# A sixth slot for x, and w2 read in full rows, in a fused attention and FFN layer on eight cores

## The chip, the cores and the metric

The kernel runs on one Trainium2 chip, on its 8 cores at once. Each core works on one of the eight batch elements (4096 tokens of width 1024) with all weights, and the cores exchange nothing. The metric is device microseconds of the slowest core.

## The reference

One layer: linear attention with a norm on its output, then a quantized feed-forward net with a norm on its output, each added to its input.

```python
x = x + _layernorm(_L0_attn_ref(_layernorm(x), W_qkv, W_o))
x = x + _layernorm(_L0_ffn_ref(_layernorm(x), w1, b1, w2, b2, gamma, beta))
# attention, chunk by chunk, 16 heads of 64; k is normalized per head
qkv = x @ W_qkv
inter = einsum('bhde,bthe->bthd', S, q_c)
scores = where(causal, einsum('bthd,bshd->bhts', q_c, k_c), 0)
intra = einsum('bhts,bshd->bthd', scores, v_c)
S = S + einsum('bthd,bthe->bhde', v_c, k_c)
y = (inter + intra) @ W_o
# ffn: h = layernorm(x)*gamma+beta; out = qlinear(gelu(qlinear(h, w1, b1)), w2, b2)
def qlinear(x, w, b):
    xq, sx = act_quant(x)          # 127/max|x| of a row, rounded
    scale = 1 / mean(abs(w)); wq = clip(round(w * scale), -1, 1)
    return (xq @ wq.T) / (sx * scale) + b
```

The sizes are x 8 x 4096 x 1024, w1 4096 x 1024 and w2 1024 x 4096, all in float32. A weight can be turned into its three values only when the mean over all of it is known, so w1 and w2 are each read twice: once to be summed, once to be quantized.

## The kernel before

A core's tokens are T = 32 tiles of 128. The kernel has two phases. In the **attention phase** a loop over i = -1..31 works on three tiles at once: iteration t finishes tile t (scores, masks, `attend`, `out_proj`), projects k, q and v of tile t+1, and begins tile t+3 (`ln1`, the activation `h1`, and its transposition by DMA, `h1_tp`). The residual add `x1(t-1)` and the statistics `ln3(t-1)` of the tile before also fall in iteration t. The result of the attention half is stored to a scratch tensor in HBM (`x1s`). In the **FFN phase** a loop over the 32 tiles does ffn1 and ffn2, reads x1 back from the scratch tensor, and stores the output.

Beside the attention phase the weights w1 and w2 are prepared. Each is cut into 32 pieces of 128 x 1024 floats (512 KB). The list `plan` gives each iteration its pieces: iterations 1 to 8 only sum (five or six pieces each), 9 to 17 mix sums with the quantization of w1, 18 to 31 only quantize (three or four each, two in the last three). POOL issues the loads (`load`) and computes the lower comparison of a piece (`below`). ACT sums pieces (`piece_sum`), DVE sums some of them (`piece_vsum`) and completes each quantization (`quant_piece`), and SP issues the transposition of the quantized piece (`piece_tp`).

A piece is loaded into one of 18 buffers: two of their own (`pc`), eight that lie where w1 will stand once quantized (`pc1`), and eight where w2 will stand (`pc2`). A table that is computed when the program is built chooses the buffer that was held least recently (`held`, `where`, `prior`), and from it `load` takes the work that it must wait for. At most four loads are in flight.

The tiles of x lie in five slots, `xs[:, k % 5]`. Numbers k of 32 and more are the tiles of x1 that the FFN phase reads back. SP serves them: in iteration t it issues the store of x1 of tile t-1 (L1062), then the transposition of h1 of tile t+3 (L1021), then it waits for the landing of that store and for `ln3(t-1)` and issues the load of tile t+4 into the slot set free (L1071), and then it issues the transpositions of the iteration's quantized pieces (L1034). DVE needs tile t+4 at the start of iteration t+1, in `ln1` (L531). Before the loop SP issues the loads of tiles 0 and 1, the eight parts of wk, the rows of b1, and the loads of tiles 2 and 3 (L1050). Meanwhile POOL issues wq, wv (L1127), the eight parts of w_o (L1129), and the first pieces.

All engines run their instructions in the order in which they are written, and wait for each other through semaphores.

Of the kernel before, what the change touches and what calls it, by code (L numbers as in the profile page):

```python
# [21 lines left out]
def build(NT=4096):  # L22
# [176 lines left out]
    def before(n, h=1):  # L199
        return 2 * (n // 3) - 1 + h  # L200

    s_xld = [sem(f"x_loaded{i}") for i in range(5)]
    s_xst = [sem(f"x1_stored{i}") for i in range(5)]
# [29 lines left out]
                                            sem("ln5_r"), sem("zn"), sem("out_ready"))  # L233

# [52 lines left out]
    held = [-1] * 10 + [8] * 8  # L287
    count = [0] * 18
# [27 lines left out]

    def slot(k):
        return xs[:, k % 5]

    def loaded(k):  # L320
        return 16 * (k // 5 + 1)

    def piece_src(p):
        j = p[2]
        if p[1] == 0:
            return w1_h[j * 128:(j + 1) * 128, :]
        return (w2_h[(j // 4) * 128:(j // 4 + 1) * 128, :]
                .rearrange("p (e b n) -> p e b n", e=2, b=4)[:, :, j % 4, :])
# [4 lines left out]
    def pe_program(PE):  # L333
# [193 lines left out]
    def dve_program(V):  # L527
        def ln1(t):
            xb = slot(t)
            V.wait_ge(s_xld[t % 5], loaded(t))  # L530
# [103 lines left out]
        def front_a(t):  # L634
            V.wait_ge(s_xld[(T + t) % 5], loaded(T + t))
# [377 lines left out]
    def sp_program(SP):  # L1013
        def rows(ap, t):
            return ap[t * 128:(t + 1) * 128, :]

        def h1_tp(t):
# [19 lines left out]
        for t in range(2):  # L1037
            SP.dma_start(out=xs[:, t], in_=rows(x_h, t)).then_inc(s_xld[t], 16)
# [10 lines left out]
        for t in range(2, 4):  # L1049
            SP.dma_start(out=xs[:, t], in_=rows(x_h, t)).then_inc(s_xld[t], 16)  # L1050
# [6 lines left out]
        for i in range(-1, T):  # L1057
            t, u, f = i, i + 1, i + 3
            if t >= 1:
                n = nWO(t - 1)  # L1060
                SP.wait_ge(s_fr[n % 3], emptied(n))
                SP.dma_start(out=rows(x1_h, t - 1), in_=slot(t - 1)  # L1062
                             ).then_inc(s_xst[(t - 1) % 5], 16)
# [12 lines left out]
            for p in now[1:]:  # L1076
                piece_tp(p)
# [6 lines left out]
        SP.dma_start(out=rows(x1_h, T - 1), in_=slot(T - 1)).then_inc(s_xst[(T - 1) % 5], 16)  # L1084
        SP.wait_ge(s_xst[(T - 1) % 5], loaded(T - 1))
        SP.wait_ge(s_bn3, T)
        SP.dma_start(out=slot(T + 4), in_=rows(x1_h, 4)).then_inc(s_xld[(T + 4) % 5], 16)
# [5 lines left out]
        for t in range(T + 1):  # L1093
# [6 lines left out]
            if t >= 1:  # L1100
                SP.wait_ge(s_out, t)
                SP.dma_start(out=rows(out_h, t - 1), in_=slot(T + t - 1)
                             ).then_inc(s_ost[(t - 1) % 5], 16)
                if t + 4 < T:
                    SP.wait_ge(s_ost[(t - 1) % 5], loaded(t - 1))
                    SP.dma_start(out=slot(T + t + 4), in_=rows(x1_h, t + 4)
                                 ).then_inc(s_xld[(T + t + 4) % 5], 16)
# [8 lines left out]
        for t in range(T - 5, T):  # L1116
            SP.wait_ge(s_ost[t % 5], loaded(t))
            SP.wait_ge(s_xst[t % 5], loaded(t))


    def pool_program(GP):
# [20 lines left out]
        def load(n):  # L1142
# [13 lines left out]
            if p[1] == 1:  # L1156
                buf = buf.rearrange("p (e n) -> p e n", e=2)
# [42 lines left out]
```

## Time and profile before

| | us |
|---|---|
| median of 3 runs | 1593.38 |
| lowest, highest | 1586.81, 1600.95 |
| the profiled execution, its time | 1589.63 |
| span of its slowest core (core 4) | 1588.1 |
| span of its fastest core (core 3) | 1571.1 |
| start of the FFN loop on core 4, about | 676 |

The span is the time from a core's first instruction to its last, and 1.5 us of the profiled time lie outside it. The profile names engines PE (TensorE matmul), PEld (its weight load), DVE (VectorE), ACT (ScalarE), POOL (GpSimd) and SP (SyncE). Iteration t of the attention loop can be found in the trace by the two DVE instructions L551, the residual add of tile t-1. The attention phase takes some 43% of the time, and the FFN phase, with PE busy nearly throughout, the rest. "DMA share" in a row is the mean busy share of the core's 16 DMA engines.

### The profile page before, as it was taken

The numbers are of one execution on the slowest core, as the hardware profiler recorded it, in microseconds if no ns is written. First come the engines' busy times: TensorE is split into PE (matmuls) and PEld (weight loads), VectorE is DVE, ScalarE is ACT, GpSimd is POOL, SyncE is SP. The second block draws the span as 40 slices with busy tenths as digits, with TensorE's granted clock in tenths as the row PEclk, the third lists the DMA queues.
The fourth block names the chain that finished last, engine by engine and source line by source line (L and its number), as shares of the span: only waits on it lengthen the run. The fifth ranks groups of instructions, "written<-read, shape, count | busy, mean of one in ns | idle before, by whom it ended". The sixth has DMA issues, their size and how long they took to land.

```text
span 1588.1 us, 26545 instructions; the slowest of 8 cores (1571.1 to 1588.1 us)
## 1 busy us (share of the span) xinstructions
PE 1461.6 (92%) x8884; PEld 726.6 (46%) x8948; DVE 1148.5 (72%) x1884; ACT 634.0 (40%) x1011; POOL 267.6 (17%) x196
## 2 busy tenths in 40 slices
PE   1589797999899999699999999999999999999997
PEld 0355454555555555334444444444444444444443
DVE  7386575777788887587767777677776777767764
ACT  1268475666465555423232232332323323233231
POOL 2002113454566775200000000000000000000000
PEclk9899898999999999899999999999999999999999
DMA  9979876768686787342433523334343342343422
GB/s 226 268 183 256 204 181 177 192 172 208 165 190 156 189 179 188 96 94 61 109 74 81 101 61 98 84 80 102 62 98 84 70 112 62 96 86 64 104 49 67
DMA packets 282277, 203.65 MB, mean 128 GB/s; under 512 B 246424, under 2 KB 246424, under 8 KB 282144
## 3 DMA queue, kind: packets, MB, share of 16 engines
q1 hardware_dynamic: 261776, 131.16, 36.2%
q0 software_dynamic: 20080, 69.74, 16.8%
q8 instruction: 74, 1.21, 0.3%
q10 hardware_dynamic: 288, 1.05, 0.3%
q14 instruction: 59, 0.48, 0.1%
HBM read 112.74 MB, written 33.55 MB: 92 GB/s over the span
## 4 chain that ended last, share of the span: by engine, by line
PE 75%; DMA 7%; DVE 4%; issue 4%; DVEq 3%; ACT 3%; POOL 1%; ACTq 1%; SPq 0%; POOLq 0%
PE pz L464 28%; PE pp L452 28%; PE pp L342 8%; PE pp L360 4%; PE pp L428 4%; DMA xs<-x 2%; DMA wv<-w_qkv 2%; DMA x1s<-xs 2%; PE pp L443 1%; POOL lt L1139 1%; DVEq L533 1%; PE pp L404 1%; DVEq L737 1%; DMA kst<-w_qkv 1%; PE pp L396 1%
## 5 line engine op out<-in xcount | busy, mean ns | idle before, releaser
L452 PE MATMUL pp<-w1p,xq1f 128*128 128x512 fp8e4 x2048 | 457.2, 382 | 0.0
L464 PE MATMUL pz<-w2p,xq2f 128*128 128x512 fp8e4 x2048 | 447.1, 379 | 0.0
L464 PEld LDWEIGHTS pz<-w2p,xq2f 128*128 128x128 bf16 x2048 | 200.4, 98 | 241.6
L452 PEld LDWEIGHTS pp<-w1p,xq1f 128*128 128x128 bf16 x2048 | 195.9, 98 | 244.1 <-issue 20.1
L678 DVE TENSOR_REDUCE st<-gsb 128x1 f32<-128x1024 f32 x128 | 152.6, 1213 | 130.3 <-ACT gsb L936 130.1
L942 ACT ACT_TABLE_LOAD x31 | 39.8, 1283 | 469.8 <-DVE st L717 469.8
L1139 POOL TENSOR_SCALAR lt<-pc,st 128x1024 bf16<-128x1024 f32 x64 | 186.1, 2910 | 31.2 <-DVE wqtp L602 15.2
L936 ACT ACTIVATE gsb<-pp,st 128x1024 f32<-128x1024 f32 x128 | 142.2, 1111 | 104.8 <-PE pp L452 99.0
L342 PE MATMUL pp<-wk,h1f 128*128 128x512 bf16 x496 | 116.4, 387 | 33.0 <-DMA h1f<-h1t 22.2
L342 PE MATMUL pp<-wv,h1f 128*128 128x512 bf16 x465 | 120.7, 404 | 20.0 <-ACT qfa L893 9.6
L1158 POOL DMA_DIRECT2D pc<-w x116 | 75.0, 647 | 333.7 <-ACT pc L928 109.3
L360 PE MATMUL pp<-h1f,wq 128*128 128x256 bf16 x1024 | 119.5, 276 | 2.7 <-DMA wq<-w_qkv 2.5
L428 PE MATMUL pp<-wo,yf 128*128 128x512 bf16 x511 | 115.8, 379 | 4.9 <-DVE wo L740 3.5
L360 PEld LDWEIGHTS pp<-h1f,wq 128*128 128x128 bf16 x1024 | 101.2, 99 | 23.1 <-issue 4.1
L700 DVE TENSOR_SCALAR xq2t<-gsb 128x1024 bf16<-128x1024 f32 x128 | 88.8, 694 | 19.0 <-issue 1.0
L602 DVE SCALAR_TENSOR_TENSOR wqtp<-pc,st,lt 128x1024 fp8e4<-128x1024 f32 x64 | 89.8, 1403 | 16.0 <-POOL lt L1139 15.7
L695 DVE TENSOR_SCALAR gsb<-gsb,st 128x1024 f32<-128x1024 f32 x128 | 95.8, 748 | 2.5
L342 PEld LDWEIGHTS pp<-wk,h1f 128*128 128x128 bf16 x512 | 50.4, 99 | 92.4 <-issue 37.5
L569 DVE TENSOR_TENSOR scT<-pp,mask 128x1024 bf16<-128x1024 f32 x64 | 75.2, 1217 | 16.7 <-PE pp L371 16.6
L342 PEld LDWEIGHTS pp<-wv,h1f 128*128 128x128 bf16 x512 | 48.5, 102 | 70.7 <-issue 28.3
L710 DVE SCALAR_TENSOR_TENSOR zb<-pz,st,b2b 128x512 f32<-128x512 f32 x64 | 47.9, 748 | 40.0 <-PE pz L464 40.0
L428 PEld LDWEIGHTS pp<-wo,yf 128*128 128x128 bf16 x512 | 48.6, 98 | 58.1 <-issue 5.5
(110 smaller groups left out, 1390.3 us busy)
## 6 DMA issues: line engine op xcount, KB each, us to landing
pc<-w POOLq DMA_DIRECT2D x116, 512.0 KB, 6.7
xs<-x SPq DMA_DIRECT2D x32, 512.0 KB, 5.0
x1s<-xs SPq DMA_DIRECT2D x32, 512.0 KB, 3.6
xs<-x1s SPq DMA_DIRECT2D x32, 512.0 KB, 3.8
out<-xs SPq DMA_DIRECT2D x32, 512.0 KB, 3.0
kst<-w_qkv SPq DMA_DIRECT2D x8, 512.0 KB, 11.5
wost<-w_o POOLq DMA_DIRECT2D x8, 512.0 KB, 39.8
wq<-w_qkv POOLq DMA_DIRECT2D x1, 2048.0 KB, 22.0
```

What stands on the lines that cost most here:

```text
L342: mi = PE.matmul(half(n, h), lhsT=hf[:, kk, :], rhs=wt[:, kk, h * 512:(h + 1) * 512], start=(kk == 0), stop=(kk == 7))
L360: mi = PE.matmul(pair(n)[:, m * 256:(m + 1) * 256], lhsT=wq[:, kk, (m0 + m) * 128:(m0 + m + 1) * 128], rhs=hf[:, kk, :], start=(kk == 0), ...
L428: mi = PE.matmul(half(n, h), lhsT=yf[:, kk, :], rhs=wo[:, kk, h * 512:(h + 1) * 512], start=(kk == 0), stop=(kk == 7))
L452: mi = PE.matmul(half(n, h), lhsT=xf[:, kk, :], rhs=w1q[:, c0 // 128:c0 // 128 + 4, kk % 4, :, kk // 4], start=False, stop=(kk == 7), skip ...
L464: mi = PE.matmul(PZ[:, h * 512:(h + 1) * 512], lhsT=xq2f[:, t % 2, kk, :], rhs=w2q[:, 4 * h:4 * h + 4, kk % 16, :, kk // 16], start=(kk == ...
L569: V.tensor_tensor(out=scT[:, :, 4 * g:4 * g + 4, :], in0=pair(n).rearrange("p (a j n) -> p a j n", a=2, j=4), in1=mask[:].unsqueeze(1).uns ...
L602: V.scalar_tensor_tensor(out=wqt[:, j % 4].rearrange("p n e -> p e n"), in0=piece_buf(p)[0].rearrange("p (e n) -> p e n", e=2), scalar=c1( ...
L678: V.tensor_reduce(out=c1(amq, s), in_=gsb[:, s * 1024:(s + 1) * 1024], axis=AX.X, op=ALU.max, apply_absolute_value=True)
L695: V.tensor_scalar(out=g, in0=g, scalar1=s2, scalar2=M32, op0=ALU.mult, op1=ALU.add)
L700: V.tensor_scalar(out=xq2t[:, s * 1024:(s + 1) * 1024], in0=g, scalar1=M32, scalar2=None, op0=ALU.subtract).then_inc(s_xq2, 1)
L936: A.activation(out=gsb[:, s * 1024:(s + 1) * 1024], in_=pair(n)[:], func=AF.Gelu, scale=c1(dq1, t % 2)).then_inc(s_fr[n % 3], 2)
L1139: GP.tensor_scalar(out=lt[:, j % 2], in0=buf, scalar1=c1(nth, p[1]), scalar2=None, op0=ALU.is_lt).then_inc(s_lt, 1)
```

## The change

There are six slots for x until tile 23 is done. The sixth is the second of the two `pc` buffers, which is no buffer for pieces until then. The table `slot_no` gives each tile its slot, and `taken_from` the tile whose place it takes. Before the loop SP issues the loads of tiles 2 to 5. In the loop a tile's load is issued when the tile six before it has been stored, one iteration sooner than before, up to tile 28; from tile 29 on it is again the tile five before. Within an iteration this load now stands behind the first two transpositions of pieces. A piece of w2 is a stretch of 1024 columns, 4 KB of a row, where it was two stretches of 512 columns that lie 2048 columns apart, and ffn2 picks its chunks accordingly.

```diff
+    LEFT = 23
+    slots = [xs[:, k] for k in range(5)] + [pc[:, 1]]
+    slot_no, load_of, taken_from = list(range(6)), [0] * 6, [-1] * 6
+    oldest = 0
+    while len(slot_no) < 2 * T:
+        if oldest == LEFT:
+            assert slot_no[LEFT] == 5
+            oldest += 1
+        slot_no.append(slot_no[oldest])
+        load_of.append(0)
+        taken_from.append(oldest)
+        oldest += 1
...
     held = [-1] * 10 + [8] * 8
+    held[1] = place[plan[LEFT + 1][0]]
...
-        return (w2_h[(j // 4) * 128:(j // 4 + 1) * 128, :]
-                .rearrange("p (e b n) -> p e b n", e=2, b=4)[:, :, j % 4, :])
+        return w2_h[(j // 4) * 128:(j // 4 + 1) * 128, (j % 4) * 1024:(j % 4 + 1) * 1024]
...
-                                   rhs=w2q[:, 4 * h:4 * h + 4, kk % 16, :, kk // 16],
+                                   rhs=w2q[:, 4 * h:4 * h + 4, 4 * (kk // 8) + kk % 4, :, kk // 4 % 2],
...
+        def x_load(t):
+            SP.wait_ge(*x1_stored(t))
+            SP.wait_ge(s_bn3, t + 1)
+            for k in range(2 * T):
+                if taken_from[k] == t:
+                    SP.dma_start(out=slot(k), in_=rows(x_h, k) if k < T else rows(x1_h, k - T)
+                                 ).then_inc(loaded(k)[0], 16)
...
-        for t in range(2, 4):
-            SP.dma_start(out=xs[:, t], in_=rows(x_h, t)).then_inc(s_xld[t], 16)
+        for t in range(2, 6):
+            SP.dma_start(out=slot(t), in_=rows(x_h, t)).then_inc(s_xld[t], 16)
...
             if f < T:
                 h1_tp(f)
-            if t >= 0:
-                k = t + 4
-                if t >= 1:
-                    SP.wait_ge(s_xst[(t - 1) % 5], loaded(t - 1))
-                    SP.wait_ge(s_bn3, t)
-                SP.dma_start(out=slot(k), in_=rows(x_h, k) if k < T else rows(x1_h, k - T)
-                             ).then_inc(s_xld[k % 5], 16)
             now = [p for p in plan[t] if p[0] == "quant"] if t >= 0 else []
             for p in now[:1]:
                 piece_tp(p)
-            for p in now[1:]:
+            for p in now[1:2]:
+                piece_tp(p)
+            if t >= 1:
+                x_load(t - 1)
+            for p in now[2:]:
                 piece_tp(p)
...
+            if not used and where[p][0] == 1:
+                GP.wait_ge(*x1_stored(LEFT))
+                GP.wait_ge(s_bn3, LEFT + 1)
```

The SP queue ahead of the loop, from the rows of b1 on (`b1w`, `b1r`: b1 and its split rows), before:

```order
5 L1046 DMA b1w<-b 1x2x512 [waits constants]
6 L1046 DMA b1w<-b 1x2x512 x3
7 L1050 DMA xs<-x 128x1024 x2
8 L1054 DMA b1r<-b1hi 1x16x64 [waits b1_split]
...
18 L1021 DMA_TRANSPOSE h1f<-h1t_53 128x8x128 [waits h1]
19 L1071 DMA xs<-x 128x1024
20 L1062 DMA x1s<-xs 128x1024 [waits pair_emptied0]
```

and with the change:

```order
5 L1076 DMA b1w<-b 1x2x512 [waits constants]
6 L1076 DMA b1w<-b 1x2x512 x3
7 L1080 DMA xs<-x 128x1024 x3
8 L1080 DMA pc<-x 128x1024
9 L1084 DMA b1r<-b1hi 1x16x64 [waits b1_split]
...
19 L1051 DMA_TRANSPOSE h1f<-h1t_53 128x8x128 [waits h1]
20 L1092 DMA x1s<-xs 128x1024 [waits pair_emptied0]
```

Tiles 4 and 5 are now asked for here, the second of them into `pc`, and the load of tile 4 that stood ahead of the first store of x1 is gone.

The SP queue in iteration 26, late in the attention phase, where the tiles have five slots again, before:

```order
125 L1062 DMA x1s<-xs 128x1024 [waits pair_emptied1]
126 L1021 DMA_TRANSPOSE h1f<-h1t_53 128x8x128 [waits h1,pe_v]
127 L1071 DMA xs<-x 128x1024 [waits x1_stored0,ln3_stats]
128 L1034 DMA_TRANSPOSE w2p<-wqtp 128x4x128 [waits piece_quantized,piece_summed]
129 L1034 DMA_TRANSPOSE w2p<-wqtp 128x4x128 [waits piece_quantized] x2
```

and with the change:

```order
131 L1092 DMA x1s<-xs 128x1024 [waits pair_emptied1]
132 L1051 DMA_TRANSPOSE h1f<-h1t_53 128x8x128 [waits h1,pe_v]
133 L1064 DMA_TRANSPOSE w2p<-wqtp 128x4x128 [waits piece_quantized,piece_summed]
134 L1064 DMA_TRANSPOSE w2p<-wqtp 128x4x128 [waits piece_quantized]
135 L1044 DMA xs<-x 128x1024 [waits x1_stored1,ln3_stats]
136 L1064 DMA_TRANSPOSE w2p<-wqtp 128x4x128 [waits piece_quantized]
```

The load of tile 30, which `ln1` needs at the start of iteration 27, has moved behind two transpositions, and the second of them waits for the iteration's second quantization on DVE. In iterations 1 to 8 no piece is quantized, so there the load stands directly behind the transposition of h1, as before, and is a load for a tile one further on.

The first loads of pieces on POOL (`pc_65` are the two buffers of their own, `pc1_66` those under w1), before:

```order
7 L1129 DMA wost_50<-w_o 128x1024 x8
8 L1158 DMA pc_65<-w1 128x1024 x2
9 L1158 DMA pc1_66<-w1 128x1024 x8
10 L1158 DMA pc_65<-w1 128x1024 x2
11 L1158 DMA pc1_66<-w1 128x1024 x7
```

and with the change:

```order
7 L1155 DMA wost_50<-w_o 128x1024 x8
8 L1185 DMA pc_65<-w1 128x1024
9 L1185 DMA pc1_66<-w1 128x1024 x8
10 L1185 DMA pc_65<-w1 128x1024
11 L1185 DMA pc1_66<-w1 128x1024 x9
```

Nine loads instead of ten find a buffer that was never used, and from the tenth on each waits for a sum.

## Rows read from the trace of the kernel before

**Rows 1.** The page: span, and busy time of each engine.

```profile
span 1588.1 us, 26545 instructions; the slowest of 8 cores (1571.1 to 1588.1 us)
PE 1461.6 (92%) x8884; PEld 726.6 (46%) x8948; DVE 1148.5 (72%) x1884; ACT 634.0 (40%) x1011; POOL 267.6 (17%) x196
```

**Rows 2.** Stretches of core 4 (columns in the first row; xN are instructions).

```profile
core 4: us, PE busy (x) PEld busy (x) DVE busy (x) ACT busy (x) POOL busy (x), PEclk, DMA share, GB/s
20.00:55.00 35.00, 13.93 (x48) 6.20 (x49) 18.80 (x25) 4.72 (x7) 7.28 (x14) 0.93 1.09 182
122.00:173.00 51.00, 42.47 (x345) 25.53 (x347) 29.20 (x48) 31.75 (x69) 11.92 (x21) 1.00 0.96 253
122.00:256.00 134.00, 111.59 (x915) 66.49 (x925) 79.43 (x130) 84.55 (x179) 26.91 (x39) 0.96 0.84 213
676.00:1588.00 912.00, 899.45 (x4280) 396.20 (x4278) 669.91 (x1165) 264.94 (x252) 0.00 (x0) 1.00 0.37 82
```

**Rows 3.** The chain that ended last, around iterations 8 and 9 (start, us, what).

```profile
231.51 8.68 DMA x1s<-xs
...
240.31 11.01 DMA xs<-x
...
251.41 0.69 DVE st L531
```

**Rows 4.** L531's waits for x on cores 3, 1, 4 (us, times); span of core 1.

```profile
  DMA xs<-x: 18.7, 8
...
  DMA xs<-x: 24.2, 7
...
  DMA xs<-x: 32.0, 8
...
core 1: 1583.3 us, clock 0.981
```

**Rows 5.** Core 4's waits from 122 to 256 us (total, times, longest), and its first one.

```profile
DVE st L531 <- DMA xs<-x: 27.9, 6, 10.8
...
6.77 0.69 DVE L531 BATCH_NORM_STATS2 st<-xs 128x6 f32<-128x512 f32 x1 [3.76 <-DMA xs<-x]
```

**Rows 6.** L551 in iterations 3 to 10 (two a tile), on cores 3, 1 and 4.

```profile
L551 DVE SCALAR_TENSOR_TENSOR xs<-pp,st,xs x16: 740/746/751, 128.6 to 260.4; 128x512 f32<-128x512 f32 x16
L551 DVE SCALAR_TENSOR_TENSOR xs<-pp,st,xs x16: 741/746/752, 129.5 to 267.8; 128x512 f32<-128x512 f32 x16
L551 DVE SCALAR_TENSOR_TENSOR xs<-pp,st,xs x16: 740/746/752, 128.6 to 273.5; 128x512 f32<-128x512 f32 x16
```

**Rows 7.** DMA issues from 122 to 256 us, KB each, median us to landing.

```profile
pc<-w POOLq DMA_DIRECT2D x38, 512.0 KB, 9.0
```

**Rows 8.** PE's start on the v projection of tile 0 (start, us, instruction, idle before).

```profile
55.03 0.58 PE L342 MATMUL pp<-wv,h1f 128*128 128x512 bf16 x1 [7.54 <-DMA wv<-w_qkv]
```

**Rows 9.** Iteration 26 in order of time.

```profile
567.52 0.33 SPq L1071 DMA_DIRECT2D xs<-x  x1
568.01 6.76 SPq L1034 DMA_TRANSPOSE w2p<-wqtp  x3
568.65 1.27 DVE L602 SCALAR_TENSOR_TENSOR wqtp<-pc,st,lt 128x1024 fp8e4<-128x1024 f32 x1
...
573.42 0.68 DVE L531 BATCH_NORM_STATS2 st<-xs 128x6 f32<-128x512 f32 x1
```

**Rows 10.** Landing of x in iterations 25 to 27; pieces of w1 (374-453 us); of w2 (459-590).

```profile
DMA to landing us min/median/max: 3.8/3.9/3.9
...
DMA to landing us min/median/max: 3.6/4.6/5.2
...
DMA to landing us min/median/max: 4.2/5.2/8.1
```

**Rows 11.** The last pieces: POOL's `below` behind its load, near the end of the phase.

```profile
638.57 3.90 POOL L1139 TENSOR_SCALAR lt<-pc,st 128x1024 bf16<-128x1024 f32 x1 [6.88 <-DMA pc<-w]
647.60 2.83 POOL L1139 TENSOR_SCALAR lt<-pc,st 128x1024 bf16<-128x1024 f32 x1 [4.42 <-DMA pc<-w]
```

More of the change, by code:

```diff
@@ L200, in before @@
         return 2 * (n // 3) - 1 + h
-    s_xld = [sem(f"x_loaded{i}") for i in range(5)]
-    s_xst = [sem(f"x1_stored{i}") for i in range(5)]
+    s_xld = [sem(f"x_loaded{i}") for i in range(6)]
+    s_xst = [sem(f"x1_stored{i}") for i in range(6)]
     s_ost = [sem(f"out_stored{i}") for i in range(5)]
@@ L233, in build, with slot, loaded, x1_stored @@
                                             sem("ln5_r"), sem("zn"), sem("out_ready"))
+    LEFT = 23
[11 more added lines that the diff above has]
+    for k in range(2 * T):
+        load_of[k] = sum(1 for j in range(k + 1) if slot_no[j] == slot_no[k])
+    def slot(k):
+        return slots[slot_no[k]]
+    def loaded(k):
+        return s_xld[slot_no[k]], 16 * load_of[k]
+    def x1_stored(t):
+        return s_xst[slot_no[t]], 16 * load_of[t]
+    def out_stored(t):
+        return s_ost[t % 5], 16 * (t // 5 + 1)
     gap, hold = 12, (7, 5)
@@ L314, in q_of @@
         return qfa[:, (t // 2) % 2, j, t % 2, :] if j < 4 else qfb[:, j - 4, t % 2, :]
[L317 to L321, printed above, removed]
     def piece_src(p):
@@ L529, in ln1 @@
             xb = slot(t)
-            V.wait_ge(s_xld[t % 5], loaded(t))
+            V.wait_ge(*loaded(t))
             V.bn_stats(out=bn1[:, 0:6], in_=xb[:, 0:512])
@@ L634, in front_a @@
         def front_a(t):
-            V.wait_ge(s_xld[(T + t) % 5], loaded(T + t))
+            V.wait_ge(*loaded(T + t))
             if t == 0:
@@ L1015, in rows @@
             return ap[t * 128:(t + 1) * 128, :]
+        def x_load(t):
+            SP.wait_ge(*x1_stored(t))
+            SP.wait_ge(s_bn3, t + 1)
+            for k in range(2 * T):
+                if taken_from[k] == t:
+                    SP.dma_start(out=slot(k), in_=rows(x_h, k) if k < T else rows(x1_h, k - T)
+                                 ).then_inc(loaded(k)[0], 16)
         def h1_tp(t):
@@ L1048, in sp_program @@
                          ).then_inc(s_b1, 16)
-        for t in range(2, 4):
-            SP.dma_start(out=xs[:, t], in_=rows(x_h, t)).then_inc(s_xld[t], 16)
+        for t in range(2, 6):
+            SP.dma_start(out=slot(t), in_=rows(x_h, t)).then_inc(s_xld[t], 16)
         SP.wait_ge(s_b1s, 1)
@@ L1062, in sp_program @@
                 SP.dma_start(out=rows(x1_h, t - 1), in_=slot(t - 1)
-                             ).then_inc(s_xst[(t - 1) % 5], 16)
+                             ).then_inc(x1_stored(t - 1)[0], 16)
             if f < T:
                 h1_tp(f)
-            if t >= 0:
-                k = t + 4
-                if t >= 1:
-                    SP.wait_ge(s_xst[(t - 1) % 5], loaded(t - 1))
-                    SP.wait_ge(s_bn3, t)
-                SP.dma_start(out=slot(k), in_=rows(x_h, k) if k < T else rows(x1_h, k - T)
-                             ).then_inc(s_xld[k % 5], 16)
             now = [p for p in plan[t] if p[0] == "quant"] if t >= 0 else []
@@ L1083, in sp_program @@
         SP.wait_ge(s_fr[n % 3], emptied(n))
[L1084 to L1087, printed above, removed]
+        SP.dma_start(out=rows(x1_h, T - 1), in_=slot(T - 1)).then_inc(x1_stored(T - 1)[0], 16)
+        x_load(T - 1)
         for s in range(4):
@@ L1102, in sp_program @@
                 SP.dma_start(out=rows(out_h, t - 1), in_=slot(T + t - 1)
-                             ).then_inc(s_ost[(t - 1) % 5], 16)
+                             ).then_inc(out_stored(t - 1)[0], 16)
                 if t + 4 < T:
-                    SP.wait_ge(s_ost[(t - 1) % 5], loaded(t - 1))
+                    assert taken_from[T + t + 4] == T + t - 1
+                    SP.wait_ge(*out_stored(t - 1))
                     SP.dma_start(out=slot(T + t + 4), in_=rows(x1_h, t + 4)
-                                 ).then_inc(s_xld[(T + t + 4) % 5], 16)
+                                 ).then_inc(loaded(T + t + 4)[0], 16)
             if v < T:
@@ L1116, in sp_program @@
         for t in range(T - 5, T):
-            SP.wait_ge(s_ost[t % 5], loaded(t))
-            SP.wait_ge(s_xst[t % 5], loaded(t))
+            SP.wait_ge(*out_stored(t))
+            SP.wait_ge(*x1_stored(t))
     def pool_program(GP):
@@ L1155, in load @@
                 GP.wait_ge(s_abs, nsum[o] + 1)
-            if p[1] == 1:
-                buf = buf.rearrange("p (e n) -> p e n", e=2)
             GP.dma_start(out=buf, in_=piece_src(p)).then_inc(s_ld, 16)
```

## The prediction

> **What bounds the kernel now.** I read the page first, then the stretches, the chain, and the waits of the one instruction that the change is about. The page says that PE is busy 92% of the span on core 4, and that the cores differ by 17 us [rows 1]. The stretches say where the rest lies. In the FFN phase PE is busy 899 of 912 us at a granted clock of 1.00, so nothing is to be had there, and nothing there changes. From 122 to 256 us PE is busy 111.6 of 134 us [rows 2]. That is the early attention phase, in which weights are summed beside it. The chain shows what the stretch waits for: the store of x1 of a tile, then the load of a new tile of x into the same slot, 8.7 and 11.0 us one after the other, then `ln1` on it, then the residual add that lets PE go on [rows 3]. The store and the load together are longer than the iteration leaves them.
>
> The size of it is read from the DVE instruction that waits, L531. Core 4 waits 32.0 us in 8 times, core 1 24.2, core 3 18.7 [rows 4]. Of core 4's, 27.9 us fall in six waits between 122 and 256 us, the longest 10.8; 3.8 are the very first load of the program, which the change leaves; the rest is 0.3 [rows 5]. So 28.2 us can go on core 4, and, taking off the same 3.8, 20.4 on core 1 and 14.9 on core 3.
>
> Is such a wait paid for one to one? The cores answer this, since they run the same program and differ in these waits. From the first residual add of iteration 3 to the last of iteration 10 core 3 takes 131.8 us, core 1 138.3 and core 4 144.9 [rows 6]. Less their waits that makes 116.9, 117.9 and 116.7 us. All three come to the same figure, so each microsecond of waiting there costs about one.
>
> **The change, part by part.**
>
> *The load an iteration sooner: -28.2 on core 4, -20.4 on core 1.* The load of a tile follows the store of the tile six before. The store is issued right behind the residual add, and lands after up to 8.7 us. From there `ln1` of the new tile is now due in the second iteration after, not the next. An iteration without waits is about 117 / 7 = 16.6 us (the 0.7 us of the second half of an add aside), and that is added to the time for the load. The load that came latest was 10.8 us late [rows 5] and would now come 5.8 us before it is needed, so all six waits of core 4 go. What is then late next is PE itself, at the 117 us above. The slowest core afterwards is not core 4 (1588.1 - 28.2 = 1559.9) but core 1 (1583.3 - 20.4 = 1562.9). I take core 1.
>
> *Two loads more ahead of the loop: +5.8.* Tiles 4 and 5 are asked for together with tiles 2 and 3, while the weights land, instead of in iterations 0 and 1. The DMA engines are full there: a share of 1.09 at 182 GB/s from 20 to 55 us [rows 2]. PE idles 7.5 us for wv, which lands at 55 us, and the chain goes through it [rows 8]. Two loads are 1.05 MB, and at 182 GB/s they take 5.8 us from the queue's other work. The wait for wv is the last to end, so it is paid in full. The bounds are 0, if wv's packets are served first, and 6.6 us or so, by a rate a tenth lower. I take 5.8, since x stood in this stretch beside wv before, and both were slow. On this the Trainium skill, in DMA: Bandwidth & Descriptors, section "Rules for kernel authors", says that DMAs issued from different engines all run on the same 16 DMA engines and interleave, so that spreading them adds no bandwidth. The row with the share of 1.09 agrees. A reader who thought that x on SP's queue could not hold up wv on POOL's would put 0 here, and reach a sum 5.8 lower.
>
> *The load behind two transpositions: +2.* Up to tile 28 the extra iteration covers it. Tiles 29 to 31 have five slots again and are loaded in iterations 25 to 27. In iteration 26 the second quantization ends at 569.9 us, and SP needs its transposition first, of three that took 6.8 us with their waits; I put one at 1.5 us. So the load is issued at 571.4 instead of 567.5, lands after 3.9 us [rows 10] at 575.3, and `ln1` at 573.4 waits 1.9 us [rows 9]. Three such waits would be 6. PE is close to being the bound there, and part of each is slack of the residual add, so I take 2 of 0 to 6. The transpositions themselves are issued a little sooner; nobody waits for that.
>
> *A piece buffer less until tile 23: +2.* The sums of iterations 1 to 8 have 7 pieces of lead where they had 8, and with five or six pieces in 16.6 us a piece is some 3 us. A load takes 9.0 us there [rows 7], so 7 pieces are enough. In iterations 17 to 20 the table of buffers gives leads of 2 to 4 pieces where it gave 4 to 7. Three or four pieces in an iteration make 4 us or more for each, and the loads take 3.6 to 5.2 us [rows 10]. Two pieces are 8 us, which still covers a load. POOL is stopped sooner by a full table, and takes DVE with it now and then: bounds 0 and 5, and I take 2.
>
> *w2 in rows of 4 KB: 0.* Pieces of w2 land after 5.2 us, of w1 after 4.6 [rows 10]. If all of the difference is due to the two half rows, each load is 0.6 us shorter. Loads are waited for only at the very end, where POOL waits 6.9 and 4.4 us for the last two [rows 11], and there DVE and PE have w1's results and the last attention tile to do. At most two times 0.6 comes out. The matmuls of ffn2 have the same shapes, so no change there.
>
> The sum on core 1: 1583.3 - 20.4 + 5.8 + 2 + 2 = 1572.7 us. With 1.5 us outside the span that is 1574.2, against 1589.6 of the same execution. The median of the runs before, 1593.4, stands 3.8 above that execution, as such waits vary from run to run. Fewer waits should leave less of that, so I add 1: **1575 us**.
>
> **The rivals.**
>
> *The DMA engines give part of it back: 1582.* The engines have a share of 0.96 at 253 GB/s from 122 to 173 us, and 0.84 over all of 122 to 256 us, where 213 GB/s x 134 us = 28.6 MB pass [rows 2]. Without the waits these bytes are wanted in 106 us, or 270 GB/s. At 253 they take 113. Then 7 us of the gain are missing. For it: the share. Against: 38 loads of pieces fall in the stretch, and run ahead of their use, so they can be late without harm. The Trainium skill, in the same page, section "Where 436 GB/s comes from", names some 358 GB/s as what HBM gives a core when its neighbour streams too. By that figure 28.6 MB would take 80 us, an estimate, and this rival would have no ground; the trace shows full engines at 253, far below it, and I go by the trace.
>
> *The wait only changes its name: 1598.* The pieces, or the transpositions of h1, become late in place of x: the sum and the quantization run on the engines that x waited on. Then only the costs are left: 1589.6 + 5.8 + 2 = 1597.4, or 1598, slower than before. It decides where the engines cannot move the bytes of one iteration (five pieces, a load and a store of x, 3.7 MB) in less time than with waits, some 20 us, or 183 GB/s. The 253 GB/s at a share of 0.96 speaks against it.
>
> *A table too small: 1622.* In iterations 17 to 20 eleven loads have the shorter leads. If each landed late enough for POOL to stand as for the last piece, 4.4 us [rows 11], that were 48 us, all on DVE's order. It needs landings over 8 us, where the longest row is 5.2 [rows 10].
>
> *The change does not do what it says: 1595, which is 1589.6 + 5.8.* That would be so if the load of x were held back on SP. In iterations 1 to 8, where the waits are, SP has no piece to transpose, so only a late store could do it. I give it next to nothing.
>
> *More than I count: 1566.* The prologue costs nothing, or the clock, 0.96 in the stretch [rows 2], comes back to 1.00.
>
> **How the numbers follow.** My forecast, 1567 to 1577, has 0.50. The partial gain, 1577 to 1588, has 0.27. More than counted, 1558 to 1567, has 0.07. The changed name, with the change that does nothing, 1592 to 1602, has 0.12, and the small table 0.04. The range 1562 to 1594 leaves out the last case, most of the one before it and half of the case of more, less than 2 in 10. One per cent is about what a measurement here tells from no change, and from 1593.4 that puts the bounds at 1577.4 and 1609.3. Faster by more has the first and the third case, 0.57; slower by more has the small table, 0.04; 0.39 is left within.
>
> **What would show it.** Right: L531 waits for x only at the start, some 4 us; the stretch of rows 6 takes 117 to 121 us on every core; wv lands at about 61 us instead of 55; the cores differ by less than 8 us. `ln1` of tiles 29 to 31 waits up to 2 us each. Wrong: if the stretch keeps its length and another instruction waits for a DMA in it; if wv still lands at 55 us; if POOL or DVE waits for pieces before iteration 25.

## The result, and the profile after

| | us |
|---|---|
| before, median of 22 runs | 1594.21 (1585.03 to 1791.16) |
| changed, median of 22 runs | 1584.47 (1578.94 to 1711.10) |
| ratio | 0.9943, 95% interval 0.992 to 0.9966 |
| changed, span of the profiled execution | 1585.2, cores 1568.9 to 1585.2 |

Both medians include a few runs in which the cores of one die had a lower clock; ratios, here and below, leave those out.

The change makes the kernel 0.6% faster. 1.2% was forecast, with 1575 us and a range of 1562 to 1594, which holds the result. The gain is half of the one that was forecast, and the likeliest case, 1567 to 1577, is missed; the rival "the DMA engines give part of it back" had said 1582.

Waits of L553, which is `ln1` in the changed kernel, for x, on core 5, its slowest, and on core 1 (us, times):

```profile
  DMA xs<-x: 9.5, 3
...
  DMA xs<-x: 7.9, 4
```

They answer to 18.7 to 32.0 us in [rows 4]. Of core 5's 9.5 us, 3.0 are the first load, and 6.5 are two waits at 547 and 569 us, where the kernel before had none. From 100 to 530 us no core waits for x at all. Stretches of core 5, against [rows 2]:

```profile
core 5: us, PE busy (x) PEld busy (x) DVE busy (x) ACT busy (x) POOL busy (x), PEclk, DMA share, GB/s
20.00:55.00 35.00, 12.03 (x48) 5.67 (x48) 17.89 (x24) 4.72 (x7) 7.83 (x14) 0.88 1.09 192
122.00:173.00 51.00, 48.68 (x425) 29.20 (x420) 36.58 (x58) 39.68 (x83) 10.91 (x21) 1.00 0.94 257
122.00:256.00 134.00, 120.11 (x1041) 71.78 (x1036) 88.71 (x141) 93.48 (x194) 27.67 (x43) 0.96 1.03 225
```

PE is busy 120.1 of the 134 us, not 111.6. But the DMA share has gone from 0.84 to 1.03, at 225 GB/s: the engines are full (in the mean of the eight cores it went from 0.83 to 0.98). What they now deliver late stands in the core's waits from 100 to 270 us, and in its DMA issues (KB each, median us to landing), against [rows 7]:

```profile
PE pp L382 <- DMA h1f<-h1t: 10.4, 2, 6.6
```

```profile
pc<-w POOLq DMA_DIRECT2D x40, 512.0 KB, 10.7
xs<-x SPq DMA_DIRECT2D x6, 512.0 KB, 9.9
x1s<-xs SPq DMA_DIRECT2D x6, 512.0 KB, 9.7
...
h1f<-h1t SPq DMA_TRANSPOSE x7, 16.5
```

The kernel before had 9.0 us for h1f in that stretch:

```profile
x1s<-xs SPq DMA_DIRECT2D x6, 512.0 KB, 7.1
xs<-x SPq DMA_DIRECT2D x6, 512.0 KB, 7.6
h1f<-h1t SPq DMA_TRANSPOSE x6, 9.0
```

The transposition of h1 is what PE's q projection (L382) reads in the next iteration. The chain of core 5 goes through it, where it went through the store and the load of x [rows 3]:

```profile
184.75 21.27 DMA h1f<-h1t
206.26 3.78 PE pp L382 x17
```

PE idles 6.6 us for it, and its granted clock falls in the wait: from 203.9 to 210.7 us it is at the lower of its two levels, 1.2 GHz, 4.4 us of them after PE has gone on (PEclk is the third value from the end):

```profile
185.00:206.00 21.00, 14.70 (x121) 7.41 (x119) 16.46 (x25) 13.36 (x27) 2.64 (x5) 0.95 1.18 217
206.00:230.00 24.00, 22.73 (x190) 14.52 (x192) 10.76 (x23) 14.51 (x31) 4.23 (x8) 0.90 1.02 220
```

The start on the v projection, against [rows 8], and iteration 26, which has five slots, against [rows 9]:

```profile
58.30 2.29 PE L364 MATMUL pp<-wv,h1f 128*128 128x512 bf16 x5 [9.20 <-DMA wv<-w_qkv]
```

```profile
559.40 1.27 DVE L624 SCALAR_TENSOR_TENSOR wqtp<-pc,st,lt 128x1024 fp8e4<-128x1024 f32 x1
560.74 1.17 SPq L1064 DMA_TRANSPOSE w2p<-wqtp  x1
...
562.07 0.46 SPq L1044 DMA_DIRECT2D xs<-x  x1
...
569.46 0.69 DVE L553 BATCH_NORM_STATS2 st<-xs 128x6 f32<-128x512 f32 x1 [5.29 <-DMA xs<-x]
573.63 1.41 DVE L573 SCALAR_TENSOR_TENSOR xs<-pp,st,xs 128x512 f32<-128x512 f32 x2
...
575.19 0.40 PE L393 MATMUL pp<-qfa,kf 64*128 64x128 bf16 x8 [3.41 <-DVE xs L573]
```

The load is issued behind two transpositions and is 5.3 us late, and PE in turn idles 3.4 us for the residual add.

The table below is the main reading of all runs. It takes from each profile the start of the residual add of some iterations (L551 before), and gives the time between them as the mean of the eight cores. The short stretch from iteration 1 to 3 (34 to 36 us) and the time from iteration 29 on, most of it the FFN phase (978 to 980 us), are left out.

| kernel | to it. 1 | 3 to 10 | 10 to 18 | 18 to 24 | 24 to 29 | mean span | ratio to before (95%) |
|---|---|---|---|---|---|---|---|
| before | 93.4 | 138.1 | 145.6 | 107.6 | 84.2 | 1581.7 | 1 |
| changed | 96.7 | 123.0 | 143.9 | 108.2 | 91.7 | 1576.5 | 0.9943 (0.992-0.9966) |
| e4, rows alone | 93.7 | 126.8 | 142.2 | 106.6 | 83.6 | 1565.5 | 0.9937 (0.9906-0.9968) |
| e5, slots alone | 97.0 | 125.3 | 149.9 | 109.1 | 93.1 | 1587.0 | 1.0028 (0.9999-1.0057) |
| e1 | 96.6 | 120.8 | 144.0 | 108.2 | 82.9 | 1565.0 | 0.9895 (0.987-0.9919) |
| e2 | 93.2 | 121.0 | 144.0 | 108.1 | 92.2 | 1571.3 | 0.9936 (0.9911-0.996) |
| e3 | 93.3 | 123.5 | 143.9 | 108.2 | 83.0 | 1564.5 | 0.9878 (0.9849-0.9907) |
| e6 | 93.0 | 119.6 | 143.9 | 108.0 | 82.9 | 1559.7 | 0.9863 (0.9831-0.9895) |
| e9 | 93.7 | 119.6 | 143.3 | 108.0 | 84.2 | 1561.5 | 0.9868 (0.9835-0.9902) |
| e10 | 93.5 | 118.3 | 143.2 | 108.0 | 84.7 | 1561.0 | 0.9833 (0.9813-0.9854) |
| e13 | 93.3 | 124.8 | 144.9 | 109.1 | 85.7 | 1572.2 | 0.9921 (0.9906-0.9936) |
| e12 | 94.6 | 138.3 | 148.9 | 108.5 | 84.2 | 1588.6 | 1.0068 (1.0044-1.0093) |
| e11 | 93.5 | 141.6 | 149.6 | 106.9 | 83.7 | 1590.0 | 0.9996 (0.9974-1.0018) |
| e8 | 94.0 | 139.3 | 192.9 | 123.7 | 96.8 | 1660.0 | 1.0532 (1.0498-1.0566) |

The changed kernel's row names three of its four parts: +3.3 us at the start, -15.1 in iterations 3 to 9, +7.5 in iterations 24 to 28. A profile is one execution, so a column can be off by some us; the ratios rest on four and more runs each. In the row of e5, iterations 10 to 17 are longer on two cores that had a lower clock, as said there.

The third column holds the clock too. Before, PE idled 17.2 us in iterations 3 to 9 in the mean of the cores (gaps over 1 us), and its clock was at 1.2 GHz for 16.6 us. In the changed kernel it was 6.5 and 4.7 us, in e10 2.8 and 0.9. In the changed kernel and in e1, e2, e3, e6, e9 and e10, cores whose clock never fell there take 117.6 to 120.5 us, and the others up to 131.2. So such a wait can cost more than its own length. Core 5 waited 10.4 us for h1f and core 6 0.6, and they differ by 13.6 us; how the rest divides was not measured.

### The profile page after: what moved, and what is told of

It reads as the page before. It is cut to its first block, busy times and chain, and to the rows that moved or that the text cites. A ratio compares the mean times of both kernels' runs of the same rounds, so it can differ in the third digit from the quotient of the medians.

```text
span 1585.2 us, 26612 instructions; the slowest of 8 cores (1568.9 to 1585.2 us)
## 1 busy us (share of the span) xinstructions
PE 1465.1 (92%) x8948; PEld 726.4 (46%) x8948; DVE 1145.8 (72%) x1884; ACT 633.9 (40%) x1011; POOL 253.7 (16%) x196
## 4 chain that ended last, share of the span: by engine, by line
PE 78%; DMA 7%; DVE 4%; issue 3%; ACT 3%; DVEq 3%; ACTq 1%; POOL 1%; SPq 0%; POOLq 0%
PE pz L486 28%; PE pp L474 28%; PE pp L364 9%; PE pp L382 5%; PE pp L450 4%; DMA h1f<-h1t 2%; DMA wv<-w_qkv 2%; PE pp L465 1%; PE pp L426 1%; DVEq L555 1%; DVEq L759 1%; DMA kst<-w_qkv 1%; PE pp L418 1%; PE pz L405 1%; DMA xs<-x 1%
## 5 line engine op out<-in xcount | busy, mean ns | idle before, releaser
L364 PE MATMUL pp<-wv,h1f 128*128 128x512 bf16 x512 | 128.8, 397 | 16.2 <-DMA wv<-w_qkv 9.2
L382 PE MATMUL pp<-h1f,wq 128*128 128x256 bf16 x1024 | 122.1, 280 | 17.3 <-DMA h1f<-h1t 10.4
L382 PEld LDWEIGHTS pp<-h1f,wq 128*128 128x128 bf16 x1024 | 102.4, 100 | 39.0 <-issue 19.1
L1185 POOL DMA_DIRECT2D pc<-w x116 | 63.8, 550 | 341.2 <-ACT pc L950 124.7
L624 DVE SCALAR_TENSOR_TENSOR wqtp<-pc,st,lt 128x1024 fp8e4<-128x1024 f32 x64 | 88.0, 1377 | 15.7 <-POOL lt L1165 15.4
```

What stands on the lines that cost most here:

```text
L364: mi = PE.matmul(half(n, h), lhsT=hf[:, kk, :], rhs=wt[:, kk, h * 512:(h + 1) * 512], start=(kk == 0), stop=(kk == 7))
L382: mi = PE.matmul(pair(n)[:, m * 256:(m + 1) * 256], lhsT=wq[:, kk, (m0 + m) * 128:(m0 + m + 1) * 128], rhs=hf[:, kk, :], start=(kk == 0), ...
L624: V.scalar_tensor_tensor(out=wqt[:, j % 4].rearrange("p n e -> p e n"), in0=piece_buf(p)[0].rearrange("p (e n) -> p e n", e=2), scalar=c1( ...
```

## The experiments

### The order in the last iterations, and the start

The theory after the result: the gain is there, and is given back at two places. e1 has the load of x first again from iteration 25 on:

```diff
+            if t > LEFT + 1:
+                x_load(t - 1)
-            if t >= 1:
+            if 1 <= t <= LEFT + 1:
                 x_load(t - 1)
```

> The changed kernel, but from iteration 25 on the load of x stands ahead of the transpositions of pieces again, as in the kernel before. Theory A: the load behind two transpositions costs the 5 us by which iterations 24 to 26 and the 2.6 us by which 27 and 28 are longer in the trace after (mean of the eight cores), since PE has no slack there. So this kernel is about 7 us faster than the changed one, some 1577, and L553 waits for x after 500 us on no core. Rival B: these waits (5 to 11 us on DVE) are mostly slack of DVE, and the iterations are longer for the POOL queue's shorter leads; then it gains 0 to 2 us, and iterations 24 to 28 stay near 92 us.

Measured: 0.9895. The iterations from 24 to 28 take 82.9 us, and `ln1` waits for x only at the start. The ratio to the changed kernel is 0.9895 / 0.9943 = 0.995, or 8 us. Theory A holds.

e2 asks for tiles 4 and 5 in iteration 0, not ahead of the loop:

```diff
-        for t in range(2, 6):
+        for t in range(2, 4):
...
+            if t == 0:
+                for k in range(4, 6):
+                    SP.dma_start(out=slot(k), in_=rows(x_h, k)).then_inc(s_xld[k], 16)
```

> The changed kernel, but tiles 4 and 5 of x are asked for in iteration 0 and not ahead of the loop. Theory A: wv lands at 53 to 55 us again, not at 55 to 58, the first residual add comes 3.3 us sooner (93.4 us as the mean of the cores, not 96.7), and the kernel is about 3 us faster than the changed one. Rival B: the engines are full from 20 to 150 us, so these two loads only delay the pieces and transpositions of iterations 0 to 3, and iteration 3 starts when it did: 0 us.

Measured: 0.9936. In the trace the first residual add comes at 93.2 us, 3.5 sooner, and the head start lasts to iteration 3. The ratio cannot tell 3 us from none. PE's start on wv on this kernel's slowest core, core 1 (58.30 above was on core 5; in the mean of the cores it was 53.7 us before, 57.1 in the changed kernel, and is 53.6 here):

```profile
53.59 3.57 PE L364 MATMUL pp<-wv,h1f 128*128 128x512 bf16 x8 [7.62 <-DMA wv<-w_qkv]
```

e3 is both edits.

> Both edits together. Theory A: the two costs are at different places and add, so 10 to 11 us below the changed kernel, some 1574, and 1.2% below the kernel before. Rival B: what is gained ahead of the loop is lost again in iterations 3 to 9, where the transpositions of h1 are late on full DMA engines: 7 us or less, 1577 or more.

Measured: 0.9878, some 10 us below the changed kernel, as theory A has it. By the means of one trace each it is theory B's: e3 and e1 are 0.5 us apart, and iterations 3 to 9 take 123.5 us, with PE waiting 4.4 us for h1f in the mean of the cores. Which of the two holds for the 3 us of the start stays open; the 8 us of the tail are sure.

e8 asks what the order costs by itself. It is the kernel before with the load of x behind the first two transpositions of pieces, as the changed kernel has it, and five slots throughout.

```diff
+            for p in now[:2]:
+                piece_tp(p)
             if t >= 0:
                 k = t + 4
...
-            for p in now[:1]:
-                piece_tp(p)
-            for p in now[1:]:
+            for p in now[2:]:
                 piece_tp(p)
```

> The kernel before with five slots and half rows, in which only the load of x is moved behind the first two transpositions of pieces. Theory A: where no iteration is left to cover it the later load is paid in nearly every iteration from 9 to 27, 2 to 5 us each, as in iterations 24 to 28 of the changed kernel: 30 to 60 us slower, 1625 to 1655. Rival B: it was paid in the changed kernel only because SP also waits there behind later work; then less than 10 us.

Measured: 1.0532, 85 us slower, above theory A's range and far from B's. The waits of L531 on its slowest core:

```profile
  DMA xs<-x: 104.0, 25
```

In iterations 10 to 17 two pieces are quantized in an iteration (three in 10 and 17), so the second transposition mostly stands for the last of them. The load is issued 9.5 us after the store has landed, where it was 0.1 before, in the mean of the cores, and these iterations take 192.9 us instead of 145.6. The clock has a part in it: in them it was at 1.2 GHz for 49 us in the mean of the cores, against 2 before. What part is waiting and what part clock was not separated.

### The two parts apart

e4 is the kernel before with w2's pieces in full rows, and nothing else.

```diff
-        return (w2_h[(j // 4) * 128:(j // 4 + 1) * 128, :]
-                .rearrange("p (e b n) -> p e b n", e=2, b=4)[:, :, j % 4, :])
+        return w2_h[(j // 4) * 128:(j // 4 + 1) * 128, (j % 4) * 1024:(j % 4 + 1) * 1024]
...
-                                   rhs=w2q[:, 4 * h:4 * h + 4, kk % 16, :, kk // 16],
+                                   rhs=w2q[:, 4 * h:4 * h + 4, 4 * (kk // 8) + kk % 4, :, kk // 4 % 2],
```

> The kernel before with nothing but the pieces of w2 in full rows of 4 KB. Theory A: no change to be measured (within 2 us of the kernel before): loads of w2 take 4.2 to 8.1 us to land before and about 0.5 us less after, and only the last few are waited for. Rival B: the shorter loads and the POOL issue of 0.53 instead of 0.76 us relieve iterations 10 to 31, and 3 to 5 us of the whole gain of 9.7 are from here.

Measured: 0.9937. I had expected nothing, in the prediction too, and theory B's 3 to 5 us are the lower end: it is 0.3 to 0.9%, the whole of what both parts give together. Its issues in 122 to 256 us on its slowest core, core 2 (columns as above; those of the kernel before are from core 4):

```profile
pc<-w POOLq DMA_DIRECT2D x40, 512.0 KB, 5.6
x1s<-xs SPq DMA_DIRECT2D x7, 512.0 KB, 4.0
xs<-x SPq DMA_DIRECT2D x7, 512.0 KB, 4.7
h1f<-h1t SPq DMA_TRANSPOSE x7, 4.3
```

Everything lands sooner, and the load of x with it. But the 9.0 and 5.6 us for a piece compare two cores, and hold pieces of w1 too, which both kernels read alike. By the order of the loads they can be told apart, on all eight cores: in this stretch the median landing of a sum's piece of w2 goes from 8.1 to 5.9 us, and of w1 from 7.0 to 6.5.

The packets show the same. The loads of w2 begin at 149 to 159 us. A 4 KB packet of POOL's queue took 203 ns in both kernels from 100 to 150 us, where only w1 is loaded, and from 170 to 256 us it took 245 ns before and 206 in e4 (mean of the cores). The rows are all that differs between the two kernels, so the half rows take more of the engines' time for the same bytes. That x lands sooner for this reason fits it; it was not shown apart. The way from a residual add over the store and the load to the landing of x took 13.7 us in the mean of iterations 3 to 9 of all cores before (1.5 to the store's issue, 5.3 for the store, 0.1, and 6.8 for the load). In e4 it takes 11.8. What an iteration leaves for it is about 12.3 us: 16.5 less the 4.2 from `ln1` to the next residual add (569.46 to 573.63 above). So a piece of w2 that lands sooner by a quarter of its time takes away half of the waits for x that the sixth slot was made for: from 100 to 530 us they are 12.0 us in the mean of the cores, and were 22.5.

e5 is the changed kernel with the half rows again.

> The changed kernel with w2's pieces read as two half rows of 2 KB again: the slots and the order of loads alone. Theory A: the two parts add. The rows alone gave a ratio of 0.9937 to the kernel before and both parts together 0.9943, so the slots alone give about 1.000, 1592 to 1596: their gain of 15 us in iterations 3 to 9 is eaten by the 3 us at the start and the 7 us in iterations 24 to 28 and by the rest. Rival B: the parts overlap, since both take away the same waits for x in iterations 5 to 9; then the slots alone also give 5 to 10 us, 1584 to 1589.

Measured: 1.0028, 0.9999 to 1.0057. Theory A holds: the slots alone give nothing that can be told from zero. The profile must be read with care. On cores 4 and 5 the granted clock was 0.81 from 254 to 414 us, with PE busy nearly throughout; in no other profile was it at that level for more than 4 us. The row of core 4, and of core 3 for comparison:

```profile
254.00:414.00 160.00, 158.16 (x1152) 89.59 (x1167) 106.66 (x160) 95.21 (x197) 62.33 (x42) 0.81 0.64 163
254.00:414.00 160.00, 149.40 (x1291) 89.35 (x1290) 118.78 (x180) 101.79 (x213) 76.28 (x51) 0.98 0.73 186
```

These two cores take 164 us for iterations 10 to 17 and the other six 145, which alone makes 4.7 us of the mean. On the six others the slots win 13.2 us in iterations 3 to 9 and 0.7 in 10 to 17, and lose 3.7 at the start, 1.5 in 18 to 23 and 8.8 in 24 to 28. That adds to nothing, and their mean span is 1580.4 us in both kernels.

### What took the place of the waits for x

PE's waits for h1f between 100 and 270 us are 0.8 us before, in the mean of the cores, and 4.9 after (0.6 to 10.4). Two theories: the pieces fill the engines too far ahead of their use, or the transposition stands behind a load and a store of x in SP's own queue. Before, `ln1` waited for x, so that load had always landed when the next transposition was issued. In the changed kernel it is still under way in 26 of the 56 cases of iterations 3 to 9 on all cores. e6 allows three loads of pieces in flight, not four:

```diff
-            if n >= 4:
-                GP.wait_ge(piece_buf(loads[n - 4])[1], piece_buf(loads[n - 4])[2])
+            if n >= 3:
+                GP.wait_ge(piece_buf(loads[n - 3])[1], piece_buf(loads[n - 3])[2])
```

> The kernel of e3 (load of x first from iteration 25 on, tiles 4 and 5 in iteration 0) with at most three loads of pieces in flight instead of four. Theory A: the transpositions of h1 land late (9 to 15 us in the mean, up to 22) because the piece loads fill the engines far ahead of their use; with three in flight PE waits for h1f 0 to 2 us instead of 4.4 (mean of the cores), and the kernel is 2 to 4 us faster than e3. Rival B: they are late for their own queue, behind a store and a load of x; then nothing changes, and the pieces of iterations 28 to 31, which are loaded just in time, may cost 0 to 3 us.

e9 issues the transposition of h1 ahead of the store of x1:

```diff
+            if f < T:
+                h1_tp(f)
             if t >= 1:
                 n = nWO(t - 1)
...
-            if f < T:
-                h1_tp(f)
```

> The kernel of e3 with the transposition of h1 issued ahead of the store of x1 on SP. Theory B of the run before: the transpositions are late since a load and a store of x of 512 KB each stand ahead of them in the same queue. Taking one of the two away shortens their landing from 9 to 15 us by 3 to 5 us, PE's wait for h1f falls from 4.4 to about 1 us, and the kernel gains 2 to 3 us on e3. If the pieces of the other queue are the cause, the landing stays within 1 us, and the store, which then starts later, may cost up to 2 us.

Measured: 0.9863 and 0.9868, and both theories are right. The median landing of h1f from 122 to 256 us, on all cores, was 6.2 us before and 10.8 in the changed kernel; it is 11.3 in e3, 7.2 in e6 and 7.7 in e9. PE's wait for h1f is 0.0 in e6 and 0.4 us in e9 in the mean, and both take 119.6 us for iterations 3 to 9. In e6's list of waits from 100 to 270 us the only one for a DMA is POOL's own:

```profile
POOL pc L1188 <- DMA pc<-w: 94.2, 33, 10.0
```

The ratios alone could not tell either from e3 (0.9878); the traces can. e10 is both together.

> The kernel of e3 with both e6 and e9: at most three loads of pieces in flight, and the transposition of h1 ahead of the store of x1. Each of them alone brought PE's waits for h1f to 0 or 0.4 us in the mean and the stretch from iteration 3 to 10 to 119.6 us. Theory A: they take away the same wait, so together they give no more than either: iterations 3 to 10 stay at 117 to 120 us, and the ratio to the kernel before at 0.986. Rival B: something of the full engines is left in iterations 3 to 17 and the two add: 0.983 or less.

Measured: 0.9833, 0.9813 to 0.9854, which is at the border between A and B: the stretch is theory A's, 118.3 us, and the ratio is B's. It is the best of all kernels run, 28 us below the kernel before as the median of its runs says (1566.91 against 1594.47 us). Its cores differ by 4.8 us, where they differed by 17 [rows 1]. That is part of the gain, since the slowest core is the metric: the mean span is 20.7 us shorter, the slowest core's 25.4. A stretch of it:

```profile
core 7: us, PE busy (x) PEld busy (x) DVE busy (x) ACT busy (x) POOL busy (x), PEclk, DMA share, GB/s
122.00:256.00 134.00, 129.90 (x1102) 77.29 (x1101) 97.38 (x156) 101.21 (x211) 31.92 (x45) 0.99 0.89 243
```

PE is busy 129.9 of 134 us, so the stretch has little more to give, at a DMA share of 0.89 and more bytes a second than before.

### Is the sixth slot needed then?

e11 is the kernel before with the full rows, three loads in flight and the transposition first, but five slots and the old order.

> The kernel before, with five slots and its order of the load of x, but with w2 in full rows, at most three loads of pieces in flight, and the transposition of h1 ahead of the store of x1. It asks what the sixth slot is worth once the engines are relieved. Theory A: the waits for x fall in the same saturated iterations 3 to 9 and shrink with the pieces' loads; what is left of them is 3 to 6 us on a core, so this kernel stands 3 to 6 us above e10, at a ratio of 0.988 to 0.990. Rival B: store and load of x in a row need more than an iteration gives them whatever the pieces do; then the waits stay at 10 us or more, and the ratio is 0.993 as with the rows alone.

Measured: 0.9996. Both missed the ratio: it is as slow as the kernel before, and worse than the rows alone. Rival B's waits of 10 us or more are there: 26.4 us for x from 100 to 270 us in the mean of the cores. Its way from the residual add to the landing of x is 14.6 us, 2.8 more than e4's. e12 takes one of the edits alone on the kernel before, the transposition first.

> The kernel before with nothing but the transposition of h1 issued ahead of the store of x1. With five slots the way from a residual add through the store and the load of x to ln1 is what iterations 3 to 9 wait for: 13.7 us in the mean before, 11.8 with w2 in full rows, 14.6 in e11. Theory A: the transposition ahead of the store makes that way about 1 to 2 us longer, in 7 iterations and a few later ones, so this kernel is 5 to 15 us slower than the kernel before, 1598 to 1608, and explains why e11 lost what the rows alone had given. Rival B: e11 lost it to the limit of three loads in flight, which moves the loads of pieces into later iterations; then this kernel is within 3 us of the kernel before or faster.

Measured: 1.0068, 11 us slower, as theory A has it. With five slots the store lies on that way, and its issue comes 2.4 us after the add, not 1.5. But the account is only half borne out. The way is 14.3 us, 0.6 longer and not 1 to 2, and in this trace iterations 3 to 9 take what they took before (138.3 and 138.1 us); 10 to 17 take 3.3 us more and the start 1.2. So that this edit costs is shown, and where it costs is not. What three loads in flight did in e11 was not tried alone.

The edit that takes away a wait with six slots hurts with five. So e10 against e11, 0.9833 against 0.9996 or some 26 us, says too much for the slot, since e11 carries an edit that harms it. The best kernel run with five slots is e4, at 0.9937, and e10 is some 17 us below it. How much of that is the slot, and how much the edits that go with it, was not separated.

e13 is e10 with the half rows.

> The kernel of e10 with w2's pieces read as two half rows again. In the changed kernel the full rows were worth 13 us (e5 against it). Theory A: they were worth so much because the engines were full and every wait in iterations 3 to 17 hung on landings; in e10 nothing hangs on them, so the half rows cost 0 to 5 us, a ratio of 0.983 to 0.987. Rival B: the half rows cost engine time in any case, and 10 us or more are lost here too: 0.990 or more.

Measured: 0.9921, 14 us above e10. Theory B holds. From 170 to 256 us a 4 KB packet of POOL's queue took 275 ns, and 230 in e10. No wait for x or h1f is left from 100 to 270 us, yet iterations 3 to 9 take 124.8 us. All of it is iteration 9: 21.9 us in the mean of the cores, and 15.4 in e10. On core 7 POOL, which may have three loads in flight and waits for slower ones (10.3 us from 225 to 256 us, and 2.2 on core 7 of e10), comes late to `below` of the first quantized piece, and DVE with it (start, us, instruction, idle before):

```profile
239.68 2.07 DVE L625 SCALAR_TENSOR_TENSOR wqtp<-pc,st,lt 128x1024 fp8e4<-128x1024 f32 x1 [5.97 <-POOL lt L1169]
...
243.13 0.59 PE L419 MATMUL pp<-qfa,sbd 128*128 128x128 bf16 x4 [5.97 <-DVE scT L592]
```

The clock falls there too, for 5.1 us in the mean of the cores. Iteration 9 accounts for 6.5 of the 11.2 us between the mean spans.

## Why the prediction was right or wrong

- *The load an iteration sooner, -20.4 on core 1, -28.2 on core 4.* The first half of the mechanism is right: the waits of `ln1` from 100 to 530 us are gone on all cores. They were 22.5 us in the mean, and the stretch gained 15.1. The step that failed is "what is then late next is PE itself". The next was the transposition of h1, at a price of 0 in the sum: PE's waits for it rose by 4.1 us in the mean, and are 10.4 on the slowest core, with time at the lower clock behind them. The rival "the wait only changes its name" had named these transpositions. I gave it 0.12 and argued it away by the bytes of an iteration, without the transposition among them. The cores' agreement at 117 us was true of a kernel in which x had always landed before the next transposition. With that wait removed in e10, 118.3 us are reached. A small misreading: the first load's wait is 2.9 and 3.0 us on cores 1 and 3, not the 3.8 of core 4 that I took off.
- *The slowest core.* The sum lets the cores draw together, from 17 us apart to less than 8, and this alone is some 40% of the 18 us: 4.8 us as core 1 takes the place of core 4, and 2.8 as fewer waits leave less variation. They stayed 16.3 us apart. The waits for h1f differ from 0.6 to 10.4 us between cores, and the three cores with the longest (5.8, 9.5 and 10.4) are the three slowest. In e10, without these waits, the cores are 4.8 us apart, as forecast.
- *The engines.* I set the rival at 0.27 and argued that late pieces do no harm. Nothing but POOL waited for them (DVE 0.2 us in the mean); but the other queue's transfers wait on the same engines, and that the row with 0.96 could have told me. By the Trainium skill's figure of 358 GB/s (DMA: Bandwidth & Descriptors, "Where 436 GB/s comes from") there would have been room. The traces do not agree: a share of 1.03 goes with 225 GB/s.
- *Two loads more ahead of the loop, +5.8.* Right in kind, 3.3 us measured in the mean (on core 1, 1.0 us, on core 5, 5.5). e2 takes it back in the trace; its ratio cannot tell.
- *The load behind two transpositions, +2 of 0 to 6.* The mis-sized term: 7.5 us, and 8 by e1. My own working had 1.9 us for each of three tiles and then struck two thirds as slack of PE. There was none: in the row above `ln1` leads straight to the residual add, and PE waits 3.4 us for that. And the load took 7.4 us to land there, not 3.9. Whether the transposition beside it is the reason was not tried.
- *A piece buffer less, +2.* About right if 1.7 + 1.6 us in iterations 10 to 23 between e4 and the changed kernel are its price. The moved load lies in the same iterations, and no run parts the two.
- *w2 in rows of 4 KB, 0.* Wrong, and the largest error: 10 us by e4, 14 by e5 and by e13. I priced the pieces' own landing, found them waited for only at the end, and stopped. A transfer that nobody waits for still uses the engines of those that are waited for: with full rows, and nothing else, the load of x landed after 5.6 us in the mean of iterations 3 to 9, and not 6.8.
- *The sum.* The two errors have opposite signs. The slots were forecast at -10.6 us net on core 1 and gave a ratio of 1.0028, nothing or a small loss; the rows were forecast at 0 and gave all there is. Of the 18.4 us forecast 9.7 were measured. That the result lies in the range at all is luck.

Of the signs named beforehand, the waits for x behaved as said up to iteration 24. The others failed: by the measure of rows 6 the stretch takes 118 to 132 us, not 117 to 121 on every core; PE starts on wv at 57.1 us in the mean of the cores and 58.3 on core 5, not at 61; the waits of the last tiles reach 5.3 us, not 2. And another instruction waits for a DMA in the stretch, which was the sign of being wrong.

The other rivals: no table was too small, though e13 shows POOL late for another reason; and the change did what it says.

## What to carry to other kernels

When the DMA engines are full, price a transfer by the engine time it takes, not by who waits for it, and ask of every queue what else stands in it once a wait is gone that used to empty it. Before an edit is moved behind others in an in-order queue, read where the last of them is released; if that is late in the iteration, the move costs a stall per iteration wherever no spare buffer covers it. An edit's worth is that of the kernel it is in: the transposition first cost 11 us with five slots, and with six it took away PE's waits for h1f. Half of this change hid the loss of the other until each was run alone. And where the slowest core is the metric, ask what makes the cores differ, for that is part of the gain.

## What the runs showed of the hardware that was not expected

- The same 512 KB in two runs of 2 KB a row instead of one of 4 KB took more of the DMA engines' time. Where w2 is loaded, from 170 to 256 us, a 4 KB packet took 245 ns and not 206 (before, e4), and 275 and not 230 in a second pair (e13, e10); where only w1 is loaded, 203 ns in both kernels of the first pair. The loads of w2 from 122 to 256 us landed after 8.1 us instead of 5.9 in the median, and the whole kernel became 0.6% to 0.9% slower. The record has packets of 4 KB in both forms. What in the engines or the memory makes the difference is open.
- A DMA transposition of 256 KB had the largest spread on full engines: 3.6 to 22.6 us to landing in the changed kernel from 122 to 256 us, on all cores, with a median of 10.8; before it was 3.6 to 18.3 with a median of 6.2. The loads of x took 3.7 to 16.2 us there in the changed kernel.
- PE's granted clock fell to 1.2 GHz in its waits: on core 5 of the changed kernel 4.2 us into the 6.6 us before 206.3 us, and it was still there 4.4 us after PE had gone on.
